# A decayed graph layer: parts of the sums added to the output by DMAs, the layernorm ahead of the tiles, batches of four

## The reference

```python
h = relu((x - mean(x)) / sqrt(var(x) + 1e-5))       # per row
support = h @ weight
mask = (adj != 0)
rank = cumsum(mask, axis=1); deg = rank[:, -1:]
k = minimum(deg, 100); pos = rank - (deg - k)
w = mask * where(pos > 0, 0.5 ** (k - pos), 0)
out = x + w @ support + bias
```

## Time and profile before

| | us |
|---|---|
| median of 3 runs | 232.07 (232.03 to 232.62) |
| the profiled execution | 232.5 |
| its span, first to last instruction | 230.1 |
| TensorE busy (matmul) | 201.8 |
| VectorE busy | 197.7 |
| ScalarE busy | 163.7 |
| GpSimd busy | 26.0 |
| loads of `adj`, issue to landing, median | 30.3 |

### The profile page before, as it was taken

One profiled execution on the slowest core, in us unless ns is written; L12 is line 12 of the kernel. 1 busy time (PEld: TensorE's weight loads), 2 busy tenths in 40 slices (PEclk: granted clock), 3 DMA queues, 4 the chain that ended last, 5 costly groups with the idle time before them and its releaser, 6 DMA issues.

```text
span 230.1 us, 6364 instructions
## 1 busy us (share of the span) xinstructions
PE 201.8 (88%) x2768; PEld 196.3 (85%) x2768; DVE 197.7 (86%) x227; ACT 163.7 (71%) x303; POOL 26.0 (11%) x53
## 2 busy tenths in 40 slices
PE   0005898899999999999999999999999899899994
PEld 0004885899999999999999999999999789899993
DVE  1799999997799989999979999969999999677053
ACT  2203489767877988878887878887889798787610
POOL 8921000411000010110010001000000000000000
PEclk9999999999999999999999999999999999999999
DMA  5999999999999999999999999999700000000001
GB/s 182 227 214 194 215 216 216 216 216 216 212 215 216 215 214 211 215 219 216 215 215 219 218 214 220 212 218 218 158 20 3 11 3 14 0 14 3 11 14 29
DMA packets 8074, 36.11 MB, mean 157 GB/s; under 512 B 1648, under 2 KB 3440, under 8 KB 3952
## 3 DMA queue, kind: packets, MB, share of 16 engines
q0 software_dynamic: 4608, 33.56, 70.1%
q1 hardware_dynamic: 3136, 2.10, 3.5%
q10 hardware_dynamic: 304, 0.07, 0.1%
HBM read 68.22 MB, written 1.05 MB: 301 GB/s over the span
## 4 chain that ended last, share of the span: by engine, by line
PE 71%; DVE 17%; issue 4%; DMA 4%; ACT 3%; POOL 1%; POOLq 0%
PE acc L570 31%; PE chain L563 22%; PE chain L561 13%; DVE masks L310 6%; DMA adj_b<-in_adj 4%; DVE part L316 3%; DVE powers L369 2%; PE acc L524 2%; ACT support L255 2%; DVE powers L362 2%; PE chain L549 1%; PE acc L514 1%; ACT powers L266 1%; DVE later L353 1%; DVE sums L344 1%
## 5 line engine op out<-in xcount | busy, mean ns | idle before, releaser
L266 ACT ACTIVATE powers<-chain 128x512 int16<-128x512 f32 (+1 forms) x282 | 152.3, 568 | 39.3 <-PE chain L563 31.3
L570 PE MATMUL acc<-support,powers 128*128 128x192 bf16 x1024 | 167.5, 246 | 2.8 <-issue 1.3
L563 PE MATMUL chain<-diag_own,masks 128*128 128x128 bf16 x640 | 125.6, 231 | 0.0
L561 PE MATMUL chain<-diag_past,masks 128*128 128x128 bf16 x596 | 118.5, 224 | 3.0 <-ACT powers L266 2.9
L570 PEld LDWEIGHTS acc<-support,powers 128*128 128x128 bf16 x1024 | 101.1, 102 | 4.5 <-DVE powers L369 1.7
L563 PEld LDWEIGHTS chain<-diag_own,masks 128*128 128x128 fp8e3 x640 | 91.0, 147 | 0.0
L561 PEld LDWEIGHTS chain<-diag_past,masks 128*128 128x128 fp8e3 x596 | 84.8, 145 | 5.0 <-ACT powers L266 4.7
L310 DVE TENSOR_SCALAR masks<-adj_b 128x4096 uint8<-128x4096 bf16 x32 | 72.9, 2279 | 3.8 <-DMA adj_b<-in_adj 3.8
L563 PE MATMUL chain<-diag_step,masks 128*128 128x128 bf16 x384 | 62.2, 220 | 0.0
L563 PEld LDWEIGHTS chain<-diag_step,masks 128*128 128x128 fp8e3 x384 | 52.1, 145 | 0.0
L206 POOL DMA_DIRECT2D adj_b<-in_adj x32 | 18.7, 585 | 116.3 <-DVE masks L310 111.8
(11 more groups left out here) (45 smaller groups left out, 53.0 us busy)
## 6 DMA issues: line engine op xcount, KB each, us to landing
adj_b<-in_adj POOLq DMA_DIRECT2D x32, 1024.0 KB, 30.3
x_sb<-in_x SPq DMA_DIRECT2D x2, 512.0 KB, 4.7
out<-x_sb SPq DMA_DIRECT2D x14, 64.0 KB, 2.6
out<-x_sb SPq DMA_DIRECT2D x4, 32.0 KB, 9.3
w<-in_L_gnn_weight ACTq DMA_DIRECT2D x2, 16.0 KB, 4.6
bias_b<-in_L_gnn_bias ACTq DMA_DIRECT2D x1, 32.0 KB, 4.5
```

The costliest lines, as they stand in the source:

```text
L266: nc.scalar.activation(powers[:, c, b, cols].bitcast(i16), chain[c][:, cols], ACT.Relu, bias=(MAX_NEIGH + 1) * STEP).then_inc(powers_ready ...
L561: nc.tensor.matmul(chain[c][:, at:at + P], column(n, t + 1), diag_past[:, :], start=False, stop=False, skip_group_check=True)
L563: return nc.tensor.matmul(chain[c][:, at:at + P], column(n, t), diag_own[:, :] if marked else diag_step[:, :], start=False, stop=True, ski ...
L570: return nc.tensor.matmul(acc[u % ACCS][:, k * 3 * D:(k + 1) * 3 * D], powers[:, u % FLIGHT, s + 1 if k < MARKS[u] else s, at:at + P], sup ...
```

## The change

- Tiles 0 to 26 (units 0 to 14) lose their three VectorE additions. SP copies x of these tiles to the output once, after mask 7 (`x_placed`). When a unit is done ScalarE copies middle and low out of PSUM (`take_side`), and one slot later VectorE writes high + bias into `top`. Units are joined in seven `GROUPS`; for each group GpSimd issues three DMAs that add low, middle and high to the output (`add_part`). Each waits until the one before it for the same pair of buffers has landed. The DMAs of group 0 stand behind loads 20, 21 and 22 in GpSimd's order, those of group 1 behind loads 29, 30 and 31, all others behind the last load.
- `side` and `top` have two buffers each: `take_side` of a unit in group j waits until all three DMAs of group j - 2 have landed.
- `BATCH` 8 becomes 4, `LOADS` 7 becomes 8, `RING` 10 becomes 12. 18 tiles are marked in place of 20; units 6, 9, 12 and 14 to 17 are wholly plain. `STARTS`, `LAGS` and the slots of `mask`, `halve_1` and the second `scan` move.
- The head: x's second half is loaded from ScalarE's queue, four loads of `adj` are issued ahead of GpSimd's `affine_select`, VectorE centres both halves, TensorE transposes the centred rows before slot 0 and the 1/std is multiplied into the product in PSUM (`scale`). Products begin in slot 7. `add_bias` covers five tiles, in slot 76.
- `SIGNED` is empty: `signs` is never called.

```diff
-    BATCH = 8
-    LOADS = 7
-    RING = 10
+    BATCH = 4
+    LOADS = 8
+    RING = 12
-    MARKS = [1, 1, 1, 2, 1, 2, 1, 1, 2, 1, 1, 2, 1, 1, 0, 0, 1, 1]
-    STARTS = [0, 5, 10, 15, 22, 28, 33, 39, 45, 50, 56, 62, 67, 73, 79, 84, 90, 96]
-    LAGS = [14, 10, 8, 11, 11, 11, 11, 11, 11, 11, 11, 11, 11, 11, 11, 11, 11, 8]
+    MARKS = [1, 1, 1, 1, 2, 2, 0, 2, 2, 0, 2, 2, 0, 2, 0, 0, 0, 0]
+    STARTS = [0, 5, 6, 12, 22, 26, 33, 39, 46, 51, 57, 63, 68, 74, 80, 85, 91, 97]
+    LAGS = [7, 5, 8, 9, 13, 11, 11, 13, 10, 11, 11, 12, 12, 11, 9, 11, 10, 8]
+    GROUPS = [[0, 1, 2], [3, 4], [5, 6], [7, 8], [9, 10], [11, 12], [13, 14]]
+    ADD_AT = [20, 29, 32, 32, 32, 32, 32]
...
         def _(sp):
+            sp.dma_start(half_of(x_sb, 0), ...).then_inc(x_loaded[0], 16)
+            sp.wait_ge(mask_ready, 8)
+            sp.dma_start(out_t[:, 0:ADDED, :], x_sb[:, 0:ADDED, :]).then_inc(x_placed, 16)
+            for u in range(GROUPS[-1][-1] + 1, NU):
...
         def _(pool):
+            def add_part(j, s):
+                b = j % 2
+                for u in GROUPS[j]:
+                    if s < 2:
+                        pool.wait_ge(side_taken[u % ACCS], u // ACCS + 1)
+                    else:
+                        pool.wait_ge(rows_done[u % ACCS], u // ACCS + 1)
+                if s == 0:
+                    pool.wait_ge(x_placed, 16)
+                if j >= 2 or s:
+                    pool.wait_ge(added[b], 48 * (j // 2) + 16 * s)
+                rows = rows_of_group(j)
+                n = rows.stop - rows.start
+                part = top[:, b, 0:n, :] if s == 2 else side[:, b, 1 - s, 0:n, :]
+                pool.dma_start(out_t[:, rows, :], part, accum_op=ALU.add).then_inc(added[b], 16)
...
             for n in range(4, NT):
                 load(n)
+                for j in range(len(GROUPS)):
+                    if 0 <= n - ADD_AT[j] < 3:
+                        add_part(j, n - ADD_AT[j])
+            for j in range(len(GROUPS)):
+                for s in range(3):
+                    if ADD_AT[j] + s >= NT:
+                        add_part(j, s)
...
         def _(act):
+            def take_side(u):
+                j, (b, at) = GROUP_OF[u], place(u)
+                act.wait_ge(acc_ready[u % ACCS], u // ACCS + 1)
+                if j >= 2:
+                    act.wait_ge(added[b], 48 * (j // 2))
+                nc.scalar.activation(side[:, b, :, at, :], parts_of(u)[:, :, 1:3, :].rearrange("q k s d -> q s k d"),
+                                     ACT.Copy).then_inc(side_taken[u % ACCS], 1)
...
+                for u in GROUP_OF:
+                    if g == STARTS[u] + LAGS[u] + STEPS[u]:
+                        take_side(u)
...
         def _(dve):
+            def add_bias_to_high(u):
+                j, (b, at) = GROUP_OF[u], place(u)
+                dve.wait_ge(bias_loaded, 16)
+                dve.wait_ge(side_taken[u % ACCS], u // ACCS + 1)
+                if j >= 2:
+                    dve.wait_ge(added[b], 48 * (j // 2))
+                nc.vector.tensor_tensor(top[:, b, at, :], parts_of(u)[:, :, 0, :],
+                                        bias_b[:, :].unsqueeze(1).to_broadcast([P, SIZES[u], D]),
+                                        ALU.add).then_inc(rows_done[u % ACCS], 1)
...
-                    if u >= 3 and to == 9 and FIRST[u] > 3:
+                    if u >= 3 and to == 8 and FIRST[u] > 3:
                         mask(FIRST[u])
```

More of the change, by code:

```diff
@@ L140, in gnn_decay_kernel @@
         std_ready = sem("std_ready")
-        unit_rows = sem("unit_rows")
         h_turned = sem("h_turned")
         h_t_ready = sem("h_t_ready")
[L144 to L147, removed]
+        support_ready = sem("support_ready")
+        scaled = [sem(f"scaled{i}") for i in range(4)]
+        part_taken = [sem(f"part_taken{i}") for i in range(4)]
+        part_ready = [sem(f"part_ready{i}") for i in range(4)]
         xb_ready = sem("xb_ready")
+        signs_ready = sem("signs_ready")
         mask_ready = sem("mask_ready")
@@ L211, in _ @@
                 nc.gpsimd.memset(m[:, :], 0.0).then_inc(zeroed, 1)
+            for n in range(4):
+                load(n)
             pool.wait_ge(zeroed, 6)
@@ L246, in turn_h, with part, signs @@
                 act.wait_ge(h_turned, i + 1)
-                t = 4 * BLOCKS[i]
-                nc.scalar.activation(h_t[:, t:t + 4, :], turned[i % 2][:, :].rearrange("p (a b) -> p a b", a=4),
+                nc.scalar.activation(h_t[:, 4 * i:4 * i + 4, :], turned[i % 2][:, :].rearrange("p (a b) -> p a b", a=4),
                                      ACT.Relu).then_inc(h_t_ready, 1)
[L251 to L256, removed]
+            def part(i, s):
+                if s:
+                    act.wait_ge(part_taken[i], s)
+                else:
+                    act.wait_ge(scaled[i], 1)
+                nc.scalar.activation(steps_of(support[:, :, s, :], i),
+                                     split[i][:, :].rearrange("p (r two d) -> p r two d", two=2, d=D),
+                                     ACT.Copy).then_inc(part_ready[i], 1)
+            def signs(n, j):
+                act.wait_ge(adj_loaded[n % LOADS], 16 * (n // LOADS + 1))
+                if n >= RING:
+                    u = UNIT_OF[n - RING]
+                    act.wait_ge(chain_ready[u % FLIGHT], taken_until(u) + TAKEN[u])
+                at = slice(j * N // PIECES, (j + 1) * N // PIECES)
+                nc.scalar.activation(masks[:, (n + SHIFT) % RING, at].bitcast(i8), adj_b[:, n % LOADS, at],
+                                     ACT.Sign).then_inc(signs_ready, 1)
             def weigh(u, b):
@@ L300, in _ @@
                             weigh(u, g - STARTS[u])
+                for n in SIGNED:
+                    if 0 <= g - SIGNED[n] < PIECES:
+                        signs(n, g - SIGNED[n])
+                for u in GROUP_OF:
+                    if g == STARTS[u] + LAGS[u] + STEPS[u]:
+                        take_side(u)
+                if g == 1:
+                    part(0, 0)
+                    part(1, 0)
+                    part(2, 0)
+                if g == 2:
+                    part(1, 1)
+                if g == 3:
+                    part(3, 0)
+                    part(0, 1)
+                if g == 4:
+                    part(2, 1)
+                    part(3, 1)
+                if g == 5:
+                    part(0, 2)
+                    part(2, 2)
+                if g == 6:
+                    part(1, 2)
+                    part(3, 2)
         @block.vector
@@ L305, in mask @@
             def mask(n):
+                if n in SIGNED:
+                    dve.wait_ge(signs_ready, PIECES * (1 + sum(m < n for m in SIGNED)))
+                    two = masks[:, (n + SHIFT) % RING, :].bitcast(u16)
+                    nc.vector.tensor_scalar(two, two, 0x0101, None, ALU.bitwise_and).then_inc(mask_ready, 1)
+                    return
                 dve.wait_ge(adj_loaded[n % LOADS], 16 * (n // LOADS + 1))
@@ L458, in _ @@
             halve_2(1)
+            scale(1)
             halve_3(1)
-            scan(1, 0)
-            normalize(0)
+            scale(0)
+            scale(3)
+            scale(2)
             mask(2)
             halve_1(2)
-            normalize(1)
+            scan(1, 0)
             halve_2(2)
             halve_3(2)
+            mask(3)
             scan(2, 0)
[L468 to L471, removed]
             for g in range(SLOTS + 4):
@@ L482, in _ @@
                         mask(FIRST[u] + 1)
-                    if u >= 3 and to == 6:
+                    if u >= 3 and to == 7:
                         halve_1(u)
@@ L490, in _ @@
                         scan(u, 0)
-                    if u >= 3 and to == 2 and SIZES[u] > 1:
+                    if u >= 3 and to == 3 and SIZES[u] > 1:
                         scan(u, 1)
                     done = STARTS[u] + LAGS[u] + STEPS[u]
+                    if u in GROUP_OF:
+                        if g == done + 1:
+                            add_bias_to_high(u)
+                        continue
                     if g == done:
@@ L520, in make_support, with take_off @@
                 pe.wait_ge(h_t_ready, i + 1)
-                if i >= 2:
-                    pe.wait_ge(low_ready, i - 1)
                 for q in range(4):
-                    last = nc.tensor.matmul(split[i % 2][:, q * P:(q + 1) * P], h_t[:, 4 * BLOCKS[i] + q, :],
+                    last = nc.tensor.matmul(split[i][:, q * P:(q + 1) * P], h_t[:, 4 * i + q, :],
                                             w2[:, :], start=(q == 0), stop=True, skip_group_check=True)
-                last.then_inc(split_ready, 1)
-            def take_off(i, s, ready):
-                pe.wait_ge(ready, i + 1)
-                t = 8 * BLOCKS[i]
-                nc.tensor.matmul(split[i % 2][:, :].rearrange("p (t d) -> p t d", d=D), minus[:, :],
-                                 support[:, t:t + 8, s, :], start=False, stop=True,
```

(25 more changed lines are left out.)

188 lines of the change are left out of this document (86 added, 102 removed).

## The result

| | before | after |
|---|---|---|
| median, us | 232.34 (232.03 to 232.64, 4 runs) | 261.74 (260.65 to 262.38, 4 runs) |
| the profiled execution | 232.5 | 260.65 |
| its span | 230.1 | 258.8 |

The change makes the kernel slower: ratio 1.126, 95% interval 1.122 to 1.131. The forecast was 261, range 240 to 269.

A forecast was written before the change was run, and what follows sets the result against it. Loads pace the kernel first, then TensorE with VectorE; the change adds ScalarE's wait for adding DMAs behind loads. 173.5 + 80.5 - 1.0 + 3.0 + 3.4 = 259.4 of span, 261.4 as median; forecast 261, own range 252 to 269, overall 240 to 269.

The forecast's parts named there:

- Who waits for whom: Slots 53 and 68: ScalarE's copy waits for adding DMAs behind loads in GpSimd's queue; in slot 68 or 69 three engines stop.
- How deep the queue was: GpSimd's queue: about six loads ahead of the first adding DMA of groups 0 and 1, 25 us or more to landing.
- When group 1 is complete: Load 31 lands at 171.0, the third adding DMA 2.5 us behind it; slot 68 goes on at 173.5, against 144.
- The first hole is covered: Slot 53 waits from 113 until about 128 for group 0; the second wait covers this, so it costs nothing.
- Slots 68 to the end: Slot 68 to the last product: 80.5 us for 82.7 before; 78 if all gaps go, 85 if VectorE's extra work counts.
- 3.0 - 1.0 of the sum: Restart at slot 68: plus 3.0 us for TensorE's slower restart, less 1.0 for what lies ready.
- The end: After the last product: 3.4 us of additions, store and closing.
- From span to median: Around the span lie 2.4 us, and the profiled execution is 0.4 above the median: 259.4 becomes 261.4.
- Like a store beside the loads: Adding DMAs land as stores do, 9.4 us each; group 1 complete at 160, total 248 us (241 to 251); chance 0.12.
- Quick, and nobody waits: Adding DMAs land in under 5 us each, no engine waits: total 230.2 us (227 to 233); chance 0.13.
- The adding DMA itself is slow: Each takes 10 us or more even in an empty queue; fifteen behind 173.5 end at 325 or later; chance 0.05.
- VectorE's relief: VectorE overall: 24 to 30 additions less (-8.2 us), but more floors and differences (+10); about +1 in all.

The follow-up runs named there:

- plain writes: The changed kernel with GpSimd's 21 adding DMAs writing in place of adding (output holds the last part only): 256.7 us, ratio 1.104 to the kernel before.
- SP's writes: The changed kernel with its 21 adding DMAs replaced by writing DMAs issued by SP, not GpSimd: 223.2 us, ratio 0.961 to the kernel before.
- kernel 2: The kernel before with only the change's tables (MARKS, BATCH 4, STARTS, LAGS, slots), old head, VectorE adding: 225.3 us, ratio 0.971 to the kernel before.
- side by side: The changed kernel with four buffers, adding DMAs of groups 2, 3 and 4 interleaved behind the last load: 227.7 us, ratio 0.981 to the kernel before.
- with VectorE's additions: The changed kernel without adding DMAs (GROUPS empty): VectorE adds low, middle and high for all units, SP stores: 223.7 us, ratio 0.963 to the kernel before.

## Why the prediction was right

*Who waits for whom.* Right in each link: ScalarE's copies in slots 53 and 68, the three DMAs of the group two before, GpSimd's queue, the last load. The plain writes and SP's writes show that it is the queue and not the addition.

*How deep the queue was.* Wrong for both groups, without harm. I had about six loads ahead and 25 us or more for the first part of each group. Group 0's found eight (36.5 us; `LOADS` is 8 now, and my six came from the kernel before with 7). Group 1's found four (18.2 us): I had slot 60 at 128, as before, and left out that by my own account slot 53 goes on only at 128; load 29 went out at 142.2. The time did not move with it, because load 31 stands behind the second part and the third behind load 31, and the loads' own pace sets when that one lands.

*When group 1 is complete.* Load 31 forecast at 171.0, measured 172.2; slot 68 goes on at 173.5, measured 173.0. The third part landed 0.7 us behind load 31, where I had 2.5: two errors of over 1 us against each other.

*The first hole is covered.* Slot 53 went on at 125.8 (forecast 128). The second hole began at 158 and ended with the loads, so the first cost nothing, as said.

*Slots 68 to the end.* Forecast 80.5, less 1.0 for what lies ready, and 3.0 for the slow clock; measured 250.7 - 173.0 = 77.7. The kernel with SP's writes has no hole and the same instructions: from its copy in slot 68 (141.27) to the last product (216.93) 75.7 us, and to the base of unit 13 (151.47) 10.2, against 12.2 from the restart (185.24). So the restart cost 2.0 us net, all of it before unit 13, just the 3.0 - 1.0 of the sum. The mis-sized term is the 80.5: measured 75.7, below even the 78 that I had if all gaps go. I took the gain of the tables too small there; what they are worth shows in kernel 2.

*The end.* Forecast 3.4, measured 8.1 (250.7 to 258.8): +4.7. I had group 6's DMAs end with the stores, and so they do: the last is issued at 250.80 and lands at 254.0, SP's last store at 254.4. What I had not is the 4.8 us behind GpSimd's landing, where the kernel before has 0.4 behind SP's. The errors of these two terms, -4.8 and +4.7, cancel, which is why the span met so closely (259.4 forecast, 258.8 measured). From span to median I added 2.0; it is 2.9, as the traced run is the shortest of the four. The mechanism was right, the fit of 261 to 261.7 luck.

*The rivals.* "Like a store beside the loads" was refuted: 36.5 and 18.2 us. "Quick, and nobody waits" would have given 230 by the prediction; without a wait on ScalarE the kernels that I ran take 223.2 (SP's writes) and, with the adding DMAs, 227.7 (side by side), so 230 was too high by up to 6 us: that rival kept much of the time that the tables save. "The adding DMA itself is slow" did not come about at 3.2 us each, but in the traced run with four buffers the row of fifteen was the bound, at 3.4 us each with the issue, below the 5 us at which I had it decide, because the kernel in front of it had become 30 us shorter. One small number of the prediction does not fit its others: slots 60 to 68 take 16 us by its own 128 and 144, not 15.3; nothing rests on the difference.

*VectorE's relief.* Taking 30 additions off VectorE brought nothing: with them off (SP's writes) 223.2, with them on 223.7, VectorE busy for 199.6 and 205.5 us. They lay beside TensorE's work.

## What to carry to other kernels

Before a DMA is put on a queue that streams, count what is ahead of it: here a DMA of 96 KB took 36.5 us to landing behind eight 1 MB loads (the first nearly in), 18.2 us one of 128 KB behind four, and about 9 us from another queue, and an engine that works in order passes that wait on to all others. A buffer that is freed by such a DMA must not be needed before the stream's landing; otherwise use another queue or more buffers. And change one thing at a time: tables worth 7 us went unseen under a mechanism that cost 38.

## What the runs showed of the hardware that I had not expected

- After GpSimd's last adding DMA had landed, 4.8 and 4.9 us passed to the end of the span (254.0 to 258.8, 220.6 to 225.5), against 0.4 us after SP's last store (before, and with VectorE's additions). It is GpSimd's DMA that the end follows, and not the addition: 4.8 us passed after GpSimd's last plain write too (248.1 to 252.9, though SP's last store landed only at 250.7), and 0.4 us after the last store where SP issued all of them. What the end waits for was not found.
- The issue of an adding DMA keeps GpSimd for 0.86 us, that of a plain write of the same bytes for 0.55, a load for 0.53; single issues took 2.8, 3.3 and 4.5 us while the other engines were busy. The Trainium skill, DMA: Bandwidth & Descriptors, section SWDGE vs HWDGE vs iDMA, says that GpSimd writes descriptors into SBUF state from which VectorE's two-port modes lock it out; that would fit, and no run here tried it.
- The same section says that a DMA engine takes turns between GpSimd's queue and those of SP and ScalarE. The trace fits: the 96 KB writes of group 0 from SP's queue landed in 9.3 us beside loads that took 36.9 in GpSimd's.
